# K's second subtraction ahead of the first normalisation's scales on GpSimd, and unread products on TensorE before the first expert

## What is computed

```python
def attn(q, k, v, mask, Wq, bq, Wk, bk, Wv, bv):
    Qh = (q @ Wq + bq).reshape(B, S, H, dh)
    Kh = (k @ Wk + bk).reshape(B, S, H, dh)
    Vh = (v @ Wv + bv).reshape(B, S, H, dh)
    scores = einsum('bqhd,bkhd->bhqk', Qh, Kh) / sqrt(10.0)
    scores = where(mask[:, None, None, :] == 0, -1e9, scores)
    return einsum('bhqk,bkhd->bqhd', softmax(scores), Vh).reshape(B, S, D)

def ffn(x, Wg, W1, W2, W3):
    scores = (x_flat @ Wg.T).T
    top_vals, token_idx = top_k(scores, 1024)
    token_w = softmax(top_vals)
    xg = x_flat[token_idx]
    h = silu(einsum('eic,ehc->eih', xg, W1)) * einsum('eic,ehc->eih', xg, W3)
    y = einsum('eih,ech->eic', h, W2) * token_w[..., None]
    return zeros_like(x_flat).at[token_idx.reshape(-1)].add(y.reshape(-1, c))

x = x + tanh(g_xattn[0]) * attn(layernorm(x), ctx, ctx, mask, Wq, bq, Wk, bk, Wv, bv)
x = x + tanh(g_ffn[0]) * ffn(layernorm(x), Wg, W1, W2, W3)
```

## Time and profile before

| | |
|---|---|
| time, median of 3 runs | 950.18 us (948.66 to 951.46) |
| the profiled execution's own time | 947.58 us |
| its span, first to last instruction | 945.8 us |
| TensorE matmul busy | 771.2 us (82%) |
| VectorE, ScalarE, GpSimd busy | 596.3, 542.3, 399.8 us |
| attention | to about 587 us |
| token choice, up to the first product of the experts | about 590 to 639.5 us |
| TensorE's longest wait in that stretch, behind the first picks | 4.9 us, to 633.08 us |
| experts | 639.5 us to the end |
| TensorE's granted clock, mean | 0.939 of full speed (2.4 GHz); 0.50 is 1.2 GHz |

### The profile page before, as it was taken

How to read it: one execution, slowest core, us unless ns; L and a number is a source line. 1 busy time by engine, 2 the same in 40 slices (tenths; PEclk the granted TensorE clock), 3 DMA queues, 4 the chain that set the end, 5 groups by cost and what they waited for, 6 DMA issues and landing times. The chain is left out here.

```text
span 945.8 us, 22564 instructions
## 1 busy us (share of the span) xinstructions
PE 771.2 (82%) x7256; PEld 605.0 (64%) x7256; DVE 596.3 (63%) x1481; ACT 542.3 (57%) x1065; POOL 399.8 (42%) x791
## 2 busy tenths in 40 slices
PE   4378889888888898888889774129999999999994
PEld 2356666566666566666666662016888888888984
DVE  1265877677686777768777764985574574654540
ACT  2254676576567657666766563735556555555641
POOL 4343344433533543353343112234548447457415
PEclk9698999999999999999999895558999999999997
DMA  4954785586578569657854613413545536534223
GB/s 123 245 130 125 199 216 140 172 237 146 171 206 207 159 169 247 162 166 193 228 149 126 169 49 102 146 35 119 112 113 89 110 84 114 112 64 68 46 24 45
DMA packets 98899, 130.38 MB, mean 138 GB/s; under 512 B 13648, under 2 KB 61936, under 8 KB 98800
## 3 DMA queue, kind: packets, MB, share of 16 engines
q1 hardware_dynamic: 86544, 112.48, 43.5%
q0 software_dynamic: 12288, 17.05, 11.0%
HBM read 52.10 MB, written 25.71 MB: 82 GB/s over the span
## 5 line engine op out<-in xcount | busy, mean ns | idle before, releaser
L576 ACT ACTIVATE p_t<-b_ps 128x512 f32<-128x512 f32 x256 | 147.8, 589 | 79.6 <-PE b_ps L951 78.2
L720 DVE TENSOR_REDUCE m_sb<-a_ps 128x4 f32<-128x512 f32 x256 | 165.3, 675 | 27.3 <-PE a_ps L938 27.1
L1269 POOL DMA_INDIRECT out<-y,idx_add x64 | 100.3, 1568 | 110.7 <-ACT y L1328 100.0
L938 PE MATMUL a_ps<-k_st,q_st 97*128 97x128 bf16 x1024 | 100.9, 222 | 34.6 <-DMA q_st<-q_part 34.6
L938 PEld LDWEIGHTS a_ps<-k_st,q_st 97*128 97x128 bf16 x1024 | 74.1, 99 | 67.0 <-issue 47.7
L951 PE MATMUL b_ps<-q_st,k_st 99*128 99x128 bf16 x1024 | 100.4, 221 | 13.7 <-ACT p_t L576 10.8
L1638 PE MATMUL bank<-x_hi,w_hi 128*128 128x512 f32 x256 | 101.9, 398 | 1.5 <-DVE x_lo L1485 1.5
L1638 PE MATMUL bank<-x_lo,w_hi 128*128 128x512 f32 x256 | 100.8, 394 | 0.0
L1638 PE MATMUL bank<-x_hi,w_lo 128*128 128x512 f32 x256 | 100.6, 393 | 0.0
L1506 DVE TENSOR_TENSOR act_h<-act_h,bank 128x512 f32<-128x512 f32 x64 | 44.0, 688 | 86.6 <-PE bank L1638 84.0
L1260 POOL DMA_INDIRECT xg<-rows_scratch,idx x64 | 68.2, 1065 | 60.3 <-issue 48.8
(11 more groups left out here) (207 smaller groups left out, 1760.6 us busy)
## 6 DMA issues: line engine op xcount, KB each, us to landing
k_st<-k_part SPq DMA_DIRECT2D x96, 256.0 KB, 3.7
q_st<-q_part SPq DMA_DIRECT2D x96, 256.0 KB, 5.0
w<-in_w_t SPq DMA_DIRECT2D x24, 512.0 KB, 5.0
rows_scratch<-xg SPq DMA_DIRECT2D x16, 528.0 KB, 6.0
x_in<-in_x SPq DMA_DIRECT2D x16, 512.0 KB, 5.9
c_t<-in_ctx_t SPq DMA_DIRECT2D x16, 512.0 KB, 5.7
x_res<-in_x SPq DMA_DIRECT2D x16, 512.0 KB, 4.8
out<-x SPq DMA_DIRECT2D x16, 512.0 KB, 4.7
```

The costliest lines, as they stand in the source:

```text
L576: act.activation(p_t[b.s % 2][:, 4 * q:4 * q + 4, :], b_ps[q % 2][:].rearrange("p (h s) -> p h s", s=P), ACT.Exp, scale=SCALE).then_inc(ex ...
L720: dve.tensor_reduce(m_sb[b.s % 2][:, 4 * q:4 * q + 4], a_ps[q % 2][:].rearrange("p (h s) -> p h s", s=P), AX_X, ALU.max).then_inc(max_done, 1)
L938: mm = pe.matmul(a_ps[q % 2][:, i * P:(i + 1) * P], q_st[g.p][0:A_K, h, tok], k_st[g.p][0:A_K, h, tok], start=True, stop=True)
L1269: pool.indirect_dma_start(out[:, :], bass.IndirectOffsetOnAxis(ap=idx_add[e % 2][:, st:st + 1], axis=0), y[st][:], None, compute_op=ALU.ad ...
```

## The change

There are two independent edits. In GpSimd's `step`, `ln1(g.on(2))` moves from between the two halves of K to behind both, but stays in step 1, ahead of `split_q`. It is called in 14 of the 16 groups (the last two have no group two further on). On TensorE, ten matmuls of 512 columns are added whose result nobody reads (`busy`): six behind the first picks, two between the two small products of the second pair of experts, and two behind the first transposes. The very first product of the first expert is written anew (`first_products`): it has the same six matmuls, in an order in which `w_hi*x_hi` and `w_lo*x_hi` of a half come first and wait only for that half's `x_hi`, and only `w_hi*x_lo` waits for that half's `x_lo`.

```diff
             def step(pool, b):
                 g = b.group
                 for m in range(KD):
                     if b.j == 1:
                         rest_k(g.on(1), m)
                         split_k(g.on(1), m)
-                        if m == 0:
-                            ln1(g.on(2))
                     if b.j == 2:
                         split_q(g.on(1), m)
+                if b.j == 1:
+                    ln1(g.on(2))
...
+        def first_products(f):
+            for k in range(KD):
+                pe.wait_ge(x_hi_done, k + 1)
+                for i, (w_, x_) in enumerate(((w_hi, x_hi), (w_lo, x_hi), (w_hi, x_lo))):
+                    if i == 2:
+                        pe.wait_ge(t_out, k + 1)
+                    mm = pe.matmul(h1_ps[0][:, 0:SPAN], w_[0][0][:, k, f], x_[0][:, k, 0:SPAN],
+                                   start=(k + i == 0), stop=(k == KD - 1 and i == 2))
+            return mm
...
+            if e + n == 0:
+                first_products(f).then_inc(h1_done, 1)
             if n % FT == 0:
                 pe.wait_ge(t_out, TRANS * e + KD * (h + 1))
             wait(pe, silu_done, HID * e + n - 1)
-            products(h1_ps[n % 2], e, 0, f, h).then_inc(h1_done, 1)
+            if e + n > 0:
+                products(h1_ps[n % 2], e, 0, f, h).then_inc(h1_done, 1)
...
+        def busy(ps, n):
+            for _ in range(n):
+                pe.matmul(ps[:, 0:512], same[:], slot[:, 0:512], start=True, stop=True)
...
         left(0)
         starts(0)
         picks(0, range(ST))
+        busy(t_ps[1], 6)
         left(1)
+        busy(t_ps[1], 2)
         starts(1)
         picks(1, range(0, TT))
         pe.wait_ge(s_begun, 4)
         transposes(0, 0)
         transposes(0, 1)
+        pe.wait_ge(s_pos, ST + TT)
+        busy(y_ps[1], 2)
```

## The result

The changed kernel takes 953.8 us in the median of its runs (948.0 to 958.4) and the kernel before, run beside it, 948.5 us. The ratio is 1.0055 with a 95% interval of 1.0038 to 1.0072: 5.3 us slower, where 8.8 us faster was predicted; the stated range of 934 to 951 us leaves 953.8 out. I use the traces for where the time goes, and the ratios for how much. Of the 10.1 us, 2.5 lie in groups 0 to 3, 6.9 in groups 4 to 13, and 1.1 behind SP's first K copy in group 14; 0.4 were gained ahead of the first.

What follows compares the result with a forecast made beforehand. The attention was taken as bound by the copies of `q_st`, with a GpSimd-ScalarE chain behind, and the experts by TensorE. Attention 7.0 us plus unread products 1.8 made 8.8 us: 950.18 to 941.4 us, range 934 to 951.

Steps and rivals of the forecast that it cites:

- the rival of the clock: Attention: TensorE's clock drops in longer waits for `q_st`; decides from four groups, 958 us with six; chance 0.06.
- The price of a drop: Attention: each clock drop costs 2.8 us, from 5.6 us of dense work at half pace at the experts' start.
- The attention's sum: Groups 6 to 13 gain 2.4 us, 4 and 5 3.4, 0 to 3 1.2: 7.0 us, between -4 and +12.
- the burst: SP's first `k_part` copy to the end of TensorE's `q_st` wait: 16.0 us instead of 16.2.
- `normalise`, `neg_hi`: ScalarE behind `ln1`: `normalise` starts at 327.7 us instead of 325.94, `neg_hi` comes 0.7 us later.
- the shrinking of the wait for `v_aug`: Attention: TensorE's 1.30 us wait for `v_aug` shrinks as K's half 1 comes earlier.
- The unread products: Experts' start: 1.8 us gained, with 0.6 the lower bound and 4.4 the upper.
- the early start of 0.6 us: Experts: the first real products start at 638.9 us instead of 639.53.
- the clock's earlier rise: Experts: TensorE busy from 636.09 us, so the clock rises at 641.7 instead of about 645.1.
- `ln1` comes too late: Attention: ScalarE reaches `neg_hi` later, VectorE's last maximum holds TensorE; 8 us lost, 956 us; chance 0.12.
- the predicted nil margin at the maximum: Group 8: VectorE's last maximum done at 336.4 us, against TensorE's transpose needing it at 336.45.
- the copies decide alone: Attention: ScalarE's gain is waited away at `q_st`; attention gives 0 to 2 us, about 947.5 us; chance 0.20.

Runs made afterwards that it cites:

- with the clock held: Changed kernel plus three unread products in TensorE's wait for `q_st` from the second group on; ratio 0.9893 to the kernel before, 10.2 us faster.
- the scales alone: Kernel before with only the move of `ln1` behind both halves of K, no unread products; ratio 1.0053, 5.0 us slower.
- the control: Kernel before plus three unread products in each group's wait for `q_st` from the second group on, `ln1` unmoved; ratio 0.9931, 6.6 us faster.
- the two kernels with the clock up in all of them: Changed kernel with three unread products per wait, six in two early groups, `total` later: 0.9868; kernel before with expert products and three per wait: 0.9940.
- the run alone: Kernel before with only the unread products at the experts and the rewritten first product, `ln1` unmoved; ratio 0.9966, 3.2 us faster.
- the version in which `normalise` starts 3.8 us earlier: Changed kernel with three unread products per `q_st` wait, but `ln1` between K's second `rest_k` and `split_k`; ratio 0.9963 to the kernel before.
- one product at the `exp`: Kernel before with `ln1` moved and one unread product per group ahead of the 0.75 us wait for an `exp`; ratio 1.0028, 2.7 us slower.

## Why the prediction was wrong

**The step that failed** is the rival of the clock, and in it the sentence "For most groups the waits are far too short". It was given a chance of 0.06. It rested on two waits of one trace: a drop behind 3.02 us (group 14), none behind 2.57 us (group 5). I took from them that a wait under 2.6 us is safe, and I had worked out waits of 1.7 us myself. The runs show the clock at 0.50 behind 13 of 15 waits, nine of them in the ten groups 4 to 13. The table takes 15 profiles of this study (without the two kernels in which TensorE waits for a maximum at a place of its own), and of each the 15 waits ahead of the first scores of groups 1 to 15. A drop is counted where the granted clock is under 0.9 in a slice of 1 us within 5 us behind the wait's end.

| length of the wait | waits | of them with a drop |
|---|---|---|
| none, or up to 0.6 us | 60 | 0 |
| 0.6 to 1.2 us | 40 | 1 |
| 1.2 to 1.6 us | 45 | 18 |
| 1.6 to 2.1 us | 35 | 20 |
| 2.1 to 2.7 us | 19 | 12 |
| 2.7 us or more | 26 | 24 |

It is no threshold but a chance that grows with the wait. The table mixes two kinds of kernels, though. Where no unread work stands in the wait, 33 of 52 waits of 1.2 to 2.1 us were followed by a drop; behind unread work it was 5 of 28. The waits of before in groups 6 to 13 (0.7 to 1.1 us) lie just under where it begins, and the change moved all of them to 1.3 to 1.9 us. With hindsight, an estimate: 14 groups, a drop in half to three quarters of them, 1.4 us each, is 10 to 15 us lost against the 8.8 gained, so 1 to 6 us slower, and up to 2.6 more where the second drop comes. The profile of the changed kernel can be added up so: with the clock held the ten groups take 324.2 us, nine drops of 1.4 us make it 336.8, and 337.1 was measured; for the scales alone, 325.2 and seven drops make 335.0 against 333.5.

**The price of a drop** in that rival, 2.8 us, was too high for the groups 6 to 13 (1.4 us, with 3.4 us at half clock) and right for those at either end, 2.7 and 2.5 us by the control, where the clock is down for 6.8 us.

**The attention's sum was right once the clock is held.** For groups 4 to 13 I had 3.4 + 2.4 = 5.8 us; the two kernels with the clock up in all of them differ by 5.9. It is spread otherwise: 0.5 us a group in groups 6 to 13 (32.3 against 32.8 us), and 0.8 in groups 4 and 5, not 1.7. For groups 0 to 3 I had 1.2 us and there is nothing, or a loss of 4 us where the clock is held with three products alone. In groups 6 to 13 the burst (15.9 to 16.3 us), `normalise`, `neg_hi` and the shrinking of the wait for `v_aug` came as worked out. The burst of 16.0 us in all groups did not: in the changed kernel it is 16.5 and 16.9 us in groups 4 and 5 (17.6 and 17.9 before), and in group 1 it grew from 15.8 to 17.3, and the wait there from 1.12 to 4.30 us.

**The unread products** were put at 1.8 us, and gain 1.8 us in the mean of the traces without a second drop, 3.2 (1.1 to 5.2) by the ratio of the run alone, with the early start of 0.6 us and the clock's earlier rise as predicted. What I did not follow is what TensorE meets next: it can come earlier to `total` than its partner on VectorE. The wait of 1.1 us grew to 1.74 and 1.98 us in two of five profiles, and in these the clock fell again. A rise won can be lost at the next wait.

**The other rivals.** That `ln1` comes too late is refuted: the version in which `normalise` starts 3.8 us earlier is 6.7 us slower, and the predicted nil margin at the maximum cost next to nothing: TensorE's waits for it ahead of L1022 are 0.2 us in all from 253 to 512 us. That the copies decide alone is refuted too: with the clock held the groups are 0.5 us shorter.

**What stays open.** The drops do not hang on the wait's length alone: 2.57 us in group 5 of before and 2.78 us for the maximum passed without one, and 1.37 us in group 8 of the changed kernel did not. Nor does a drop begin at one distance from the wait: with one product at the `exp` the scores at once behind the wait, at 372.58 us, are slow, in the changed kernel it is 1.5 us later. The Trainium skill, TensorE: Matmul & The Clock Gate, What's actually happening, states that the chip watches TensorE's activity in a window that runs freely, and that the number of slow matmuls at a kernel's start therefore differs from run to run. The table, in which like waits come out either way, would fit a window of that kind; no run here tested it. Its section HAM oscillation — how this bites in real kernels tells of a kernel whose clock falls anew at each tile's wait for a transfer of some 3 to 5 us; the changed kernel agrees, with a drop behind 13 of 15 waits, but most of its waits are shorter, from 1.36 us on. And that the whole change stands at +5.3 us where its parts give +1.8 is explained by the second drop only in part, and lies within what the intervals of the parts leave open.

## What to carry to other kernels

When an edit lets TensorE arrive earlier at a wait that another unit ends, the idle time moves there and grows; count the waits that pass 1.2 us (where drops begin in this kernel), and price each with a chance of a clock drop, instead of asking whether one is long enough. A gain that ends as TensorE's idle time ahead of dense work should be made together with unread products in that wait: here they turned 5 us lost into 8 to 12 us gained, of which 6.6 us came without the edit too. So try them in the kernel before as well. Place them behind the wait for the bank that they write, and only where that is surely over, or they are a wait of their own.

## What was not expected of the hardware

- Waits of 1.2 to 2.1 us on an otherwise busy TensorE were followed by some 3.4 us at a granted clock of 0.50 in 38 of 80 cases, and in 33 of 52 where no unread work stood in the wait. In the changed kernel TensorE is busy for 352 of 400 us of the attention, and the mean clock is 0.96:

```profile
120.00:520.00 400.00, 351.82 (x4037) 262.20 (x4038) 289.13 (x693) 259.73 (x537) 162.37 (x455) 0.96 0.70 181
```

- Half a microsecond of work in such a wait (1.4 to 1.9 down to 0.7 to 1.1 us) was enough for groups 6 to 13; the same work 4 to 5 us earlier was not. Waits of 1.28 to 1.60 us directly behind 1.5 us of unread work passed without a drop in all of groups 6 to 13.
- The kernel before had two drops too, at 70 and 530 us in its trace. With three unread products in each group it is 6.6 us faster; its trace shows 5.2 us of that at these two places.
